# One decoder layer in fp32: bias products of the weight fold on VectorE, first token loads behind two weights, bias columns on ScalarE's queue

## The chip, the cores and the metric

The kernel runs on one core of one Trainium2 chip. A core has TensorE (matmuls, called PE in the profile), VectorE (DVE), ScalarE (ACT), GpSimd (POOL) and SyncE (SP), and 16 DMA engines that all its DMA queues share. The metric is the device time of one execution in microseconds, as a median over runs. All data are fp32. A matmul of fp32 operands appears in the trace as two passes, so that a product over four tiles of the contraction counts 8 there; a transpose through TensorE appears once.

## The reference

x is 16 sequences of 256 tokens of width 512. The layer adds three residual branches, each behind a layer norm: self attention with three softmaxes over one score matrix, a cross attention with 8 heads and relative positions over a window, and a feed-forward part in which each token picks one of 8192 experts in each of 8 heads. Only the first part matters here:

```python
Q = x @ Wq + bq
K = x @ Wk + bk
V = x @ Wv + bv
raw = jnp.einsum('bqd,bkd->bqk', Q, K) * scale
...  # three softmaxes over raw (causal, over means of 4 keys, over the top 64)
out = (w_attn + c_attn + s_attn) / 3.0
return out @ Wo + bo
```

Since raw = (x Wq + bq)(x Wk + bk)^T, the kernel needs from the two weights and the two biases only four things: the matrix Wq Wk^T (512 x 512), the column Wk bq, the row Wq bk, and the number bq . bk.

## The kernel before

The program has a short start, 19 rounds of attention that are pipelined over the 16 sequences, and an expert stage of 32 rounds. At the start weights are folded. First, with transposes through TensorE (jobs TQ and TK, four banks each), Wq and Wk are turned; ScalarE copies each bank to `raw_q` and `raw_k`. Then four products M build `w_qk` = Wq Wk^T, one bank of 512 columns each. Job C gives the column `b_g` = Wk bq and the number `bqk` from matmuls whose moving operand is 2 columns wide (`b_q2`, bq written twice), with the transposed Wk as the weights, and job U gives the row `u_row`, Wq bk, on all 128 partitions, from a copy of bk spread over 128 columns (`b_k_wide`) against the transposed Wq. The list `FOLD_JOBS` fixes the order of these jobs and so which of four PSUM banks (`s_bank`, of which two are named h_bank) each takes: job n waits until ScalarE has emptied job n - 4. TensorE goes on to TK, and then to M, only when ScalarE has emptied all four banks of the weight before.

After the fold each engine runs `rounds`: a fixed program of 32 steps for each round, in which every engine does its part in the order that `round_` lists. Round -1 has only the first half of self attention of sequence 0 (transposes of the normalised tokens, the products Q and RAW, then at step 16 the fold of Wv and Wo with the job BO, then V and CK). Its first transposes need nothing of the fold but TensorE's turn and the normalised tokens; ScalarE copies them to `xn_t` only after it has copied `u_row`. VectorE's product of the normalised tokens with `u_row` (L1156) gives a bias of each score row.

SyncE's queue issues, in order, Wq, Wk, the seven small bias columns (semaphore `first_in`, awaited by VectorE before its first copies), Wv, Wo and the other weights. GpSimd issues the tokens of sequences 0 and 1 (`x_in`, named xn_ring in the trace), between building the identity matrix and clearing some tiles, and then the first context `c_in`. In the start VectorE spreads the bias columns, computes the statistics of sequence 0 and normalises it (L1139). GpSimd then clears `probs` (L675), whose memory held the untransposed Wq and Wk (`w_q`, `w_k`; in the trace all of it is in_rows). At steps 17 and 18 of round -1 GpSimd adds the folded output bias to the tokens of sequence 0 (`add_bo`, L579), for which it waits for job BO; the power that gives sequence 1 its reciprocal deviations (L556) stands behind it in GpSimd's program, at step 26.

Of the kernel before, what the change touches and what calls it, by code (L numbers as in the profile page):

```python
# [20 lines left out]
ALU = mybir.AluOpType  # L21
# [3 lines left out]
P = 128  # L25
# [102 lines left out]
def attention_pass(nc, w, kept_stats, early, x3_dram, rows_in, rows_out, rows_laid, fold_dram):  # L128
# [115 lines left out]
    def a_job(b, kind, n=0):  # L244
        return jobs_before(a_jobs, b) + a_jobs(b).index((kind, n))

    FOLD_JOBS = ([("TQ", m) for m in range(KD)] + [("TK", m) for m in range(KD)] + [("M", m) for m in range(KD)]
                 + [("C", 0), ("U", 0)] + [("TV", m) for m in range(KD)] + [("W", m) for m in range(KD)]
# [8 lines left out]
    with ExitStack() as ctx:  # L257
# [29 lines left out]
        b_q2 = sb("b_q2", [P, KD, 2])  # L287
        b_k_wide, b_v_wide = (sb(f"b_{n}_wide", [P, KD, P]) for n in "kv")
        b_g = sb("b_g", [P, KD])
        u_row = sb("u_row", [P, D])  # L290
# [66 lines left out]
        wide_ready = sem("wide_ready")  # L357
        row_bias_ready = sem("row_bias_ready")
# [75 lines left out]
        def _(sp):  # L434
            for n, (tile, src) in enumerate(weights):
                sp.dma_start(tile, src.rearrange("(k p) n -> p k n", p=P)).then_inc(
                    first_weight[n] if n < N_EARLY else rest_in, 16)
                if n == N_EARLY - 1:
                    for column, col_src in columns:
                        sp.dma_start(column[:], col_src).then_inc(first_in, 16)  # L440
# [95 lines left out]
        def _(pool):  # L536
# [6 lines left out]
            for b in range(2):  # L543
                pool.dma_start(x_in[:, b, :, :], w["x"][b].rearrange("(t p) n -> p t n", p=P)).then_inc(
                    x_loaded[b], 16)
# [4 lines left out]
            after(nc.gpsimd.memset(band[:], 0.0))  # L550
            pool.dma_start(c_in[:], w["ctx"][0].rearrange("(t p) n -> p t n", p=P)).then_inc(c_loaded, 16)
# [87 lines left out]
            def round_(b, p):  # L639
                for s in range(STEPS):  # L640
# [21 lines left out]
                    if norm_in_round(b):  # L662
                        if s == At.LOAD_X and not (isinstance(b, int) and b == -1):
                            load_x(b + 2, p)
                        if s == At.POWER:
                            power(mom, rstd, 0, b + 2)
                        if 0 <= s - At.ADD_BO < TT:
                            add_bo(b + 2, p, s - At.ADD_BO)
                    if isinstance(b, int) and b == -1 and 0 <= s - At.LOAD_X < TT:
                        add_bo(0, 0, s - At.LOAD_X)  # L670
# [3 lines left out]
            pool.wait_ge(f_emptied, f_job("TK", KD - 1) + 1)  # L674
            nc.gpsimd.memset(probs[:], 0.0).then_inc(probs_zeroed, 1)  # L675
# [4 lines left out]
        def _(pe):  # L680
# [196 lines left out]

            def fold_scores():

                pe.wait_ge(first_weight[0], 16)  # L880
                turn_weight("TQ", w_q)
                pe.wait_ge(first_weight[1], 16)
                turn_weight("TK", w_k)
                for m in range(KD):
                    bank = f_open("M", m)
                    product(bank[:], lambda k: raw_q[:, k, m * P:(m + 1) * P], lambda k: raw_k[:, k, :],
                            KD).then_inc(f_filled, 1)
                pe.wait_ge(wide_ready, 1)
                bank = f_open("C")
                for m in range(KD):  # L890
                    product(bank[:, 2 * m:2 * m + 2], lambda k: raw_k[:, k, m * P:(m + 1) * P],
                            lambda k: b_q2[:, k, :], KD)
                product(bank[:, 2 * KD:2 * KD + 2], lambda k: b_k_wide[:, k, :], lambda k: b_q2[:, k, :],
                        KD).then_inc(f_filled, 1)
                bank = f_open("U")
                product(bank[:], lambda k: b_k_wide[:, k, :], lambda k: raw_q[:, k, :], KD).then_inc(f_filled, 1)
# [58 lines left out]
        def _(act):  # L955
# [120 lines left out]
            def fold_scores():  # L1076
                turn_weight("TQ", raw_q)
                turn_weight("TK", raw_k)
                for m in range(KD):
                    bank = f_full("M", m)  # L1080
                    nc.scalar.copy(w_qk[:, m, :], bank[:]).then_inc(f_emptied, 1)
                bank = f_full("C")
                nc.scalar.copy(b_g[:].unsqueeze(2), bank[:, 0:2 * KD].rearrange("p (m c) -> p m c", c=2)[:, :, 0:1])
                nc.scalar.mul(bqk[:], bank[:, 2 * KD:2 * KD + 1], SCALE).then_inc(f_emptied, 1)
                bank = f_full("U")
                nc.scalar.copy(u_row[:], bank[:]).then_inc(f_emptied, 1)
# [41 lines left out]

            fold_scores()
            act.wait_ge(first_in, 16 * N_FIRST_DMAS)  # L1130
            nc.scalar.mul(cb_qs[:], cb_q[:], XSCALE)
            self_wait(act)
            act.wait_ge(f_emptied, f_job("U") + 1)
# [3 lines left out]
        def _(dve):  # L1137
# [232 lines left out]
            nc.vector.tensor_copy(b_q2[:], b_q[:].unsqueeze(2).to_broadcast([P, KD, 2]))  # L1370
            nc.vector.tensor_copy(cb_v2[:], cb_v[:].unsqueeze(2).to_broadcast([P, CT, 2]))
            nc.vector.tensor_copy(b_k_wide[:], b_k[:].unsqueeze(2).to_broadcast([P, KD, P]))
            nc.vector.tensor_copy(b_v_wide[:], b_v[:].unsqueeze(2).to_broadcast([P, KD, P])).then_inc(wide_ready, 1)
            for t in range(TT):
                norm_stats(0, 0, t)
            for t in range(TT):
                norm_x(0, 0, t)
            dve.wait_ge(f_emptied, f_job("U") + 1)
# [564 lines left out]
```

## Time and profile before

| | us |
|---|---|
| Median of three runs | 2556.84 |
| Fastest and slowest of them | 2553.26, 2561.5 |
| Span of the profiled execution | 2553.4 |
| TensorE busy, share of the span | 2402.2 (94%) |
| VectorE busy | 2042.5 (80%) |
| ScalarE busy | 1121.9 (44%) |
| GpSimd busy | 1079.4 (42%) |

The span runs from the first to the last instruction. No other time is given for the profiled execution; its span lies beside the fastest of the three timed runs. Busy is time in which an engine had an instruction in it. In the rows further down the first number is the start of a group of like instructions in us from the span's start, the second is the time the group took; in square brackets stand the idle time of the engine before it and what ended that. Among the columns of a table of stretches, PEclk is the clock that TensorE was granted, as a share of 2.4 GHz. The fold ends at 44.55 us of the span.

### The profile page before, as it was taken

How to read it: one execution, taken by the hardware profiler on the slowest of the kernel's cores; microseconds unless marked ns; L12 is line 12 of the kernel's file. 1: busy time of each engine (PE TensorE's matmuls, PEld its weight loads, DVE VectorE, ACT ScalarE, POOL GpSimd, SP SyncE). 2: the span in 40 equal slices, each digit the busy share in tenths (PEclk: the TensorE clock that was granted, in tenths of full speed). 3: DMA queues.
4: the chain of work that ended last, by engine and by line, in shares of the span. 5: the costliest groups of instructions: out<-in, count | busy, mean ns of one | idle time of the engine just before them, and what ended most of it. 6: DMA issues, size and time to landing. Idle time of an engine off the chain costs nothing. (4 is left out here: it accounts for less than half of the span.)

```text
span 2553.4 us, 40781 instructions
## 1 busy us (share of the span) xinstructions
PE 2402.2 (94%) x12856; PEld 1333.3 (52%) x12856; DVE 2042.5 (80%) x5966; ACT 1121.9 (44%) x2612; POOL 1079.4 (42%) x1564
## 2 busy tenths in 40 slices
PE   7889999999999999999989899999999999999985
PEld 5456666656666566666555344444444444444432
DVE  1467776677767776677665699999999999999997
ACT  2257666667666666667666122222122222212221
POOL 1133333333333333334233445555555555555552
PEclk9999999999999999999999999999999999999998
DMA  3035554455545545455458789999999999999996
GB/s 112 15 108 139 163 151 141 134 148 149 155 125 144 162 143 155 114 145 172 135 148 258 272 337 390 392 382 384 382 382 383 385 389 391 383 383 382 385 371 261
DMA packets 292741, 622.47 MB, mean 244 GB/s; under 512 B 162352, under 2 KB 163376, under 8 KB 292528
## 3 DMA queue, kind: packets, MB, share of 16 engines
q0 software_dynamic: 83968, 438.34, 45.2%
q1 hardware_dynamic: 174768, 80.85, 11.9%
q10 hardware_dynamic: 33792, 100.67, 11.7%
q8 instruction: 105, 1.72, 0.3%
q14 instruction: 108, 0.88, 0.1%
HBM read 577.80 MB, written 142.61 MB: 282 GB/s over the span
## 5 line engine op out<-in xcount | busy, mean ns | idle before, releaser
L1544 POOL DMA_INDIRECT out_rows<-rows_out,rows_now x256 | 272.0, 1063 | 373.1 <-PE out_ps L1611 292.5
L1054 ACT ACTIVATE in_rows<-scores,nmx 128x512 f32<-128x512 f32 x512 | 373.2, 729 | 113.8 <-DVE nmx L1243 111.1
L1565 PE MATMUL l_bank<-fold,xn_tf 128*128 128x512 f32 x960 | 421.6, 592 | 0.0
L1060 ACT COPY in_rows<-t_bank 128x512 f32<-128x512 f32 x512 | 298.7, 584 | 214.7 <-PE t_bank L715 213.7
L1535 POOL DMA_INDIRECT in_rows<-rows_in,rows_now x248 | 303.2, 1223 | 128.9 <-DVE hid L1799 63.8
L622 POOL TENSOR_TENSOR added<-mask_add,band 128x136 f32<-128x136 f32 (+1 forms) x512 | 246.7, 483 | 256.4 <-DVE nmx L1243 255.0
L715 PE MATMUL t_bank<-ident,in_rows 128*128 128x128 f32 x2048 | 319.6, 281 | 10.1 <-ACT in_rows L1027 5.1
L715 PEld LDWEIGHTS t_bank<-ident,in_rows 128*128 128x128 f32 x2048 | 237.4, 143 | 171.6 <-issue 100.8
L683 PE MATMUL a_bank<-fold 128*128 128x256 f32 (+1 forms) x1024 | 303.9, 441 | 15.4 <-ACT fold L975 6.9
L1807 DVE CUSTOM_DVE_ANT_0 out_rows<-out_rows,hid 128x1024 f32<-128x1024 f32 x256 | 307.1, 1221 | 3.5 <-ACT hid L1668 3.5
L1655 ACT COPY sims<-l_bank 128x512 f32<-128x512 f32 x120 | 70.2, 585 | 537.2 <-PE l_bank L1565 516.9
L1565 PEld LDWEIGHTS l_bank<-fold,xn_tf 128*128 128x128 f32 x960 | 182.4, 190 | 229.6 <-issue 229.6
L1243 DVE CUSTOM_DVE_ANT_0 scores<-h_bank,added 128x512 f32<-128x512 f32 x256 | 174.6, 688 | 157.8 <-PE s_bank L705 146.3
L1607 PE MATMUL out_ps<-w_out,hid_t 128*128 128x512 f32 x512 | 229.8, 602 | 10.6 <-ACT hid_t L1690 10.6
L683 PEld LDWEIGHTS a_bank<-fold 128*128 128x128 f32 x1024 | 187.5, 191 | 91.5 <-issue 49.5
L1577 PE MATMUL hid_ps<-w_in,xn_kept 128*128 128x512 f32 x512 | 226.9, 596 | 7.5 <-ACTq L1710 6.0
L1799 DVE SCALAR_TENSOR_TENSOR hid<-in_rows,lin,hid 128x1024 f32<-128x1024 f32 x160 | 204.5, 1278 | 0.5
L621 POOL COPY added<-mask_add 128x128 f32<-128x128 f32 (+2 forms) x224 | 71.6, 319 | 314.5 <-DVE nmx L1243 302.7
L1243 DVE CUSTOM_DVE_ANT_0 scores<-s_bank,added 128x512 f32<-128x512 f32 x256 | 175.5, 686 | 33.0 <-ACT in_rows L1054 11.5
L1771 DVE CUSTOM_DVE_ANT_0 in_rows<-in_rows,xn_ring 128x512 f32<-128x512 f32 x256 | 161.2, 683 | 9.6 <-PEq L257 9.6
L1577 PEld LDWEIGHTS hid_ps<-w_in,xn_kept 128*128 128x128 f32 x512 | 97.8, 191 | 131.9 <-issue 131.9
L705 PE MATMUL h_bank<-in_rows 32*128 32x512 f32 x512 | 146.0, 647 | 17.2 <-DVE nmx L1243 14.7
(210 smaller groups left out, 3829.9 us busy)
## 6 DMA issues: line engine op xcount, KB each, us to landing
rows_in<-in_in_b_dram ACTq DMA_DIRECT2D x16, 2048.0 KB, 8.5
rows_out<-in_out_a_dram ACTq DMA_DIRECT2D x16, 2048.0 KB, 9.0
rows_in<-in_in_a_dram ACTq DMA_DIRECT2D x16, 1024.0 KB, 8.3
rows_out<-in_out_b_dram ACTq DMA_DIRECT2D x16, 1024.0 KB, 5.8
rel_scratch<-rel_pad SPq DMA_DIRECT2D x16, 640.0 KB, 3.2
band<-rel_scratch SPq DMA_DIRECT2D x512, 20.0 KB, 2.5
prob_scratch<-in_rows SPq DMA_DIRECT2D x512, 20.0 KB, 2.3
near<-prob_scratch SPq DMA_DIRECT2D x64, 156.1 KB, 3.1
```

What stands on the lines that cost most here:

```text
L622: nc.gpsimd.tensor_tensor(added[:, s % 2, lo:hi], mask[:, lo:hi], band[:, group % 2, g, lo - first:hi - first], ALU.add).then_inc(added_re ...
L683: ins = nc.tensor.matmul(out, lhs(k), rhs(k), start=(k == 0), stop=(k == k_tiles - 1 and not more))
L715: ins = nc.tensor.transpose(bank[:, k * P:(k + 1) * P], src[:, k * P:(k + 1) * P], ident[:])
L1054: nc.scalar.activation(prob_tile(s % PSLOTS), scores[:, s % 2, :], ACT.Exp, bias=nmx[:, s:s + 1], scale=-1.0, accum_out=lsum[:, s:s + 1]). ...
L1060: nc.scalar.copy(prob_t[:, n // HPT % 2, n % HPT, :, :].rearrange("p k q -> p (k q)"), bank[:]).then_inc(t_emptied, 1)
L1243: nc.vector.tensor_tensor_reduce(out=scores[:, s % 2, :], in0=s_bank[s % HPT][:, 0:L], in1=added[:, s % 2, :], scale=-1.0, scalar=-NEG, op ...
L1535: nc.gpsimd.indirect_dma_start(in_rows[:, place_in(h, odd), :], None, rows_in, bass.IndirectOffsetOnAxis(rows_now[:, odd, h:h + 1], 0)).th ...
L1544: nc.gpsimd.indirect_dma_start(out_rows[:, h, :], None, rows_out, bass.IndirectOffsetOnAxis(rows_now[:, odd, h:h + 1], 0)).then_inc(out_lo ...
L1565: ins = nc.tensor.matmul(l_bank[c % 2][:], xn_t[:, k, :], fold[:, k, c * BANK:(c + 1) * BANK], start=(k == 0), stop=(k == KD - 1))
L1577: ins = nc.tensor.matmul(hid_ps[:, n * BANK:(n + 1) * BANK], xn_kept[:, k, :], w_in[:, k, n * BANK:(n + 1) * BANK], start=(k == 0), stop=F ...
L1607: nc.tensor.matmul(out_ps[:], hid_t[:, k, :], w_out[:, k, :], start=(k == 0), stop=False, skip_group_check=True)
L1807: nc.vector.tensor_tensor_reduce(out=out_a[:, h, :], in0=out_a[:, h, :], in1=hid[:], scale=1.0, scalar=0.0, op0=ALU.mult, op1=ALU.add, acc ...
```

## The change

1. The jobs C and U no longer multiply. After the first M bank TensorE transposes spread copies of bq and bk (4 transposes each, jobs BQ and BK), which puts the bias as a row on every partition; ScalarE copies the two banks to `b_q_row` and `b_k_row`. VectorE multiplies the untransposed weights with those rows and sums along them: four instructions give `u_col`, four give `b_g`, one gives `bqk`. `u_col` is spread to 128 columns and TensorE transposes it (4 transposes, the new job U).
2. The bias columns are issued from ScalarE's queue, before its first work, and not from SyncE's behind Wk.
3. GpSimd issues the tokens and `c_in` after its clearing, and only once Wq and Wk have landed.
4. GpSimd's clearing of `probs`, and ScalarE's first copy of a round, wait for `columns_ready`, since the products read and overwrite the weights in that memory. The additions of the output bias for sequence 0 move from steps 17 and 18 behind the power at step 26.

```diff
-                 + [("C", 0), ("U", 0)] + [("TV", m) for m in range(KD)] + [("W", m) for m in range(KD)]
+    FOLD_JOBS = ([("TQ", m) for m in range(KD)] + [("TK", m) for m in range(KD)] + [("M", 0), ("BQ", 0), ("BK", 0)]
+                 + [("M", m) for m in range(1, KD)] + [("U", 0)] + [("TV", m) for m in range(KD)] + [("W", m) for m in range(KD)]
...
# SyncE
-                if n == N_EARLY - 1:
-                    for column, col_src in columns:
-                        sp.dma_start(column[:], col_src).then_inc(first_in, 16)
...
# GpSimd
-            for b in range(2):
-                pool.dma_start(x_in[:, b, :, :], w["x"][b].rearrange("(t p) n -> p t n", p=P)).then_inc(
-                    x_loaded[b], 16)
             after(nc.gpsimd.memset(rel_k4[:], 0.0))
...
             after(nc.gpsimd.memset(band[:], 0.0))
+            for i in range(N_EARLY):
+                pool.wait_ge(first_weight[i], 16)
+            for b in range(2):
+                pool.dma_start(x_in[:, b, :, :], w["x"][b].rearrange("(t p) n -> p t n", p=P)).then_inc(
+                    x_loaded[b], 16)
...
                         if s == At.POWER:
                             power(mom, rstd, 0, b + 2)
+                            if b == -1:
+                                for t in range(TT):
+                                    add_bo(0, 0, t)
...
-                    if isinstance(b, int) and b == -1 and 0 <= s - At.LOAD_X < TT:
-                        add_bo(0, 0, s - At.LOAD_X)
...
             pool.wait_ge(f_emptied, f_job("TK", KD - 1) + 1)
+            pool.wait_ge(columns_ready, 1)
             nc.gpsimd.memset(probs[:], 0.0).then_inc(probs_zeroed, 1)
...
# TensorE
+            def lay_row(kind, wide):
+                bank = f_open(kind)
+                for k in range(KD):
+                    ins = nc.tensor.transpose(bank[:, k * P:(k + 1) * P], wide[:, k, :], ident[:])
+                ins.then_inc(f_filled, 1)
...
-                pe.wait_ge(wide_ready, 1)
-                bank = f_open("C")
-                for m in range(KD):
-                    product(bank[:, 2 * m:2 * m + 2], lambda k: raw_k[:, k, m * P:(m + 1) * P],
-                            lambda k: b_q2[:, k, :], KD)
-                product(bank[:, 2 * KD:2 * KD + 2], lambda k: b_k_wide[:, k, :], lambda k: b_q2[:, k, :],
-                        KD).then_inc(f_filled, 1)
-                bank = f_open("U")
-                product(bank[:], lambda k: b_k_wide[:, k, :], lambda k: raw_q[:, k, :], KD).then_inc(f_filled, 1)
+                    if m == 0:
+                        pe.wait_ge(wide_ready, 1)
+                        lay_row("BQ", b_q_wide)
+                        lay_row("BK", b_k_wide)
+                pe.wait_ge(u_ready, 1)
+                lay_row("U", u_wide)
...
# ScalarE
+                    if m == 0:
+                        for kind, row in (("BQ", b_q_row), ("BK", b_k_row)):
+                            nc.scalar.copy(row, f_full(kind)[:]).then_inc(f_emptied, 1)
+                nc.scalar.copy(u_row[:], f_full("U")[:]).then_inc(f_emptied, 1)
...
+            for column, col_src in columns:
+                act.dma_start(column[:], col_src).then_inc(first_in, 16)
             fold_scores()
...
+            act.wait_ge(columns_ready, 1)
             act.wait_ge(f_emptied, f_job("U") + 1)
             rounds(round_)
...
# VectorE
+            dve.wait_ge(f_emptied, f_job("BK") + 1)
+
+            def against_row(weight, row, scale, column):
+                return nc.vector.tensor_tensor_reduce(out=weight, in0=weight, in1=row, scale=scale, scalar=0.0,
+                                                      op0=ALU.mult, op1=ALU.add, accum_out=column)
+
+            for m in range(KD):
+                against_row(w_q[:, m, :], b_k_row, 1.0, u_col[:, m:m + 1])
+            self_wait(dve)
+            nc.vector.tensor_copy(u_wide, u_col[:].unsqueeze(2).to_broadcast([P, KD, P])).then_inc(u_ready, 1)
+            for m in range(KD):
+                against_row(w_k[:, m, :], b_q_row, 1.0, b_g[:, m:m + 1])
+            against_row(b_k_row, b_q_row, SCALE, bqk[:]).then_inc(columns_ready, 1)
+            self_wait(dve)
             dve.wait_ge(f_emptied, f_job("U") + 1)
             rounds(round_)
```

TensorE's program of the fold, before (L874 are transposes of weights, L683 products, the last row begins round -1):

```order
L874 MATMUL s_bank<-ident,in_rows 128x128 x8
L683 MATMUL h_bank<-in_rows 128x512 x8
L683 MATMUL s_bank<-in_rows 128x512 x8
L683 MATMUL h_bank<-b_q,in_rows 128x2 x16
L683 MATMUL h_bank<-b_q,b_k_wide 128x2 x4
L683 MATMUL h_bank<-in_rows,b_k_wide 128x512 x4
L743 MATMUL a_bank<-ident,fold 128x128 x8
```

The same place now (L879 transposes of weights, L688 products, L887 the rows laid, of which "fold" is where the spread bq and the spread `u_col` lie):

```order
L879 MATMUL s_bank<-ident,in_rows 128x128 x8
L688 MATMUL h_bank<-in_rows 128x512 x4
L887 MATMUL h_bank<-ident,fold 128x128 x4
L887 MATMUL s_bank<-ident,b_k_wide 128x128 x4
L688 MATMUL s_bank<-in_rows 128x512 x4
L688 MATMUL h_bank<-in_rows 128x512 x8
L887 MATMUL s_bank<-ident,fold 128x128 x4
L748 MATMUL a_bank<-ident,fold 128x128 x8
```

The 24 matmuls of C and U are gone from between M and round -1; eight transposes stand behind the first M bank and four behind the last.

VectorE's program from its spreading of the biases to its first product of a round, before (ISA is the product with a sum along the row, and the row after it the write of the sum):

```order
L1372 COPY b_k_wide<-b_k 128x512
L1373 COPY b_v_wide<-b_v 128x512
L49 BN_STATS stats<-xn_ring 128x6 x2
L53 BN_AGGR mom<-stats 128x2 x2
L55 TENSOR_SCALAR mom<-mom 128x2
L1139 TENSOR_SCALAR fold<-xn_ring,mom,rstd 128x512 x2
L1156 ISA w_in,row_bias<-fold,u_row,bqk 128x512
```

The same place now (in_rows holds Wq and Wk, xn_kept the row of bk, xn_tf that of bq):

```order
L1384 COPY b_k_wide<-b_k 128x512
L49 BN_STATS stats<-xn_ring 128x6 x2
L53 BN_AGGR mom<-stats 128x2 x2
L55 TENSOR_SCALAR mom<-mom 128x2
L1150 TENSOR_SCALAR fold<-xn_ring,mom,rstd 128x512 x2
L1392 ISA in_rows,u_col<-in_rows,xn_kept 128x512
L1392 ISA u_col 128x1
...
L1398 COPY fold<-u_col 128x512
...
L1392 ISA xn_kept,bqk<-xn_kept,xn_tf 128x512
L1392 ISA bqk 128x1
L1167 ISA w_in,row_bias<-fold,u_row,bqk 128x512
```

Nine products L1392 have come in, four ahead of the spreading of `u_col` and five behind it; all stand behind the first statistics, which wait for the tokens of sequence 0, and the first of them waits until ScalarE has emptied job BK.

## Rows read from the trace of the kernel before

**Rows 1.** Busy time of each engine in stretches (start:end, length, engines, PEclk, DMA share, GB/s).

```profile
220.00:300.00 80.00, 76.83 (x615) 49.17 (x614) 57.91 (x190) 54.25 (x134) 29.48 (x63) 1.00 0.52 147
300.00:380.00 80.00, 76.83 (x615) 49.25 (x614) 58.07 (x188) 54.33 (x136) 29.79 (x63) 1.00 0.50 145
1400.00:2500.00 1100.00, 1060.01 (x2814) 482.96 (x2814) 1057.84 (x2863) 230.97 (x420) 586.49 (x541) 0.99 0.96 375
```

**Rows 2.** TensorE in order of time: start, time, line, operation, count [idle before, ended by].

```profile
6.71 1.94 PE L874 MATMUL h_bank<-ident,in_rows 128*128 128x128 f32 x8 [6.71 <-DMA in_rows<-in_attn_Wq_dram]
...
12.72 1.94 PE L874 MATMUL h_bank<-ident,in_rows 128*128 128x128 f32 x8 [2.36 <-issue]
...
17.04 9.61 PE L683 MATMUL h_bank<-in_rows 128*128 128x512 f32 x16 [0.67 <-ACT in_rows L1074]
26.48 7.03 PE L683 MATMUL s_bank<-in_rows 128*128 128x512 f32 x16
33.35 4.67 PE L683 MATMUL h_bank<-b_q,in_rows 128*128 128x2 f32 x32
...
39.58 5.13 PE L683 MATMUL h_bank<-in_rows,b_k_wide 128*128 128x512 f32 x8
44.55 0.60 PE L743 MATMUL a_bank<-ident,fold 128*128 128x128 f32 x4
...
60.40 1.04 PE L874 MATMUL s_bank<-ident,in_rows 128*128 128x128 f32 x8
...
77.32 3.60 PE L683 MATMUL s_bank<-in_rows,b_v_wide 128*128 128x512 f32 x8
...
96.30 0.60 PE L743 MATMUL a_bank<-ident,fold 128*128 128x128 f32 x4
```

**Rows 3.** Stretches around the end of the fold, columns as in Rows 1.

```profile
35.00:40.00 5.00, 5.00 (x27) 5.00 (x27) 0.00 (x0) 0.24 (x2) 0.00 (x0) 0.57 0.00 0
40.00:45.00 5.00, 5.00 (x12) 2.12 (x11) 0.00 (x0) 0.25 (x1) 0.00 (x0) 0.75 0.00 0
```

**Rows 4.** DMA issues of the start: size of one, us from issue to landing.

```profile
in_rows<-in_attn_Wq_dram SPq DMA_DIRECT2D x1, 1024.0 KB, 5.8
in_rows<-in_attn_Wk_dram SPq DMA_DIRECT2D x1, 1024.0 KB, 11.4
xn_ring<-in_x_dram POOLq DMA_DIRECT2D x2, 512.0 KB, 8.6
...
b_q<-in_attn_bq_dram SPq DMA_DIRECT2D x1, 2.0 KB, 11.3
...
cb_o<-in_xattn_bo_dram SPq DMA_DIRECT2D x1, 1.0 KB, 9.5
```

**Rows 5.** Two stretches of one us in the loading, columns as in Rows 1.

```profile
11.00:12.00 1.00, 0.00 (x0) 0.00 (x0) 0.00 (x0) 0.00 (x0) 0.00 (x0) 1.00 1.04 362
12.00:13.00 1.00, 0.28 (x2) 0.31 (x3) 0.00 (x0) 0.00 (x0) 0.00 (x0) 1.00 0.84 165
```

**Rows 6.** VectorE in order of time.

```profile
15.22 0.42 DVE L1372 COPY b_k_wide<-b_k 128x512 f32<-128x512 f32 x1
...
15.89 1.28 DVE L49 BATCH_NORM_STATS2 stats<-xn_ring 128x6 f32<-128x512 f32 x2
...
18.66 4.21 DVE L1139 TENSOR_SCALAR fold<-xn_ring,mom,rstd 128x512 f32<-128x512 f32 x2 [0.92 <-POOL rstd L556]
45.37 0.75 DVE L1156 CUSTOM_DVE_ANT_0 w_in<-fold,u_row,bqk 128x512 f32<-128x512 f32 x1 [22.50 <-ACT u_row L1086]
...
85.66 0.55 DVE L1139 TENSOR_SCALAR fold<-xn_ring,mom,rstd 128x512 f32<-128x512 f32 x1 [10.40 <-POOL rstd L556]
```

**Rows 7.** ScalarE in order of time, at the end of U.

```profile
44.75 0.59 ACT L1086 COPY u_row<-h_bank 128x512 f32<-128x512 f32 x1 [4.76 <-PE h_bank L683]
...
45.57 0.58 ACT L975 COPY fold<-a_bank 128x512 f32<-128x512 f32 x1
```

**Rows 8.** GpSimd in order of time, the clearing and the first output bias.

```profile
18.59 3.55 POOL L675 MEMSET in_rows<- 128x4160 f32 x1
...
82.48 2.48 POOL L579 TENSOR_TENSOR xn_ring<-xn_ring,b_o 128x512 f32<-128x512 f32 x2 [20.07 <-ACT b_o L1094]
```

More of the change, by code:

```diff
@@ L245, in a_job @@
         return jobs_before(a_jobs, b) + a_jobs(b).index((kind, n))
-    FOLD_JOBS = ([("TQ", m) for m in range(KD)] + [("TK", m) for m in range(KD)] + [("M", m) for m in range(KD)]
-                 + [("C", 0), ("U", 0)] + [("TV", m) for m in range(KD)] + [("W", m) for m in range(KD)]
+    FOLD_JOBS = ([("TQ", m) for m in range(KD)] + [("TK", m) for m in range(KD)] + [("M", 0), ("BQ", 0), ("BK", 0)]
+                 + [("M", m) for m in range(1, KD)] + [("U", 0)] + [("TV", m) for m in range(KD)] + [("W", m) for m in range(KD)]
                  + [("BO", 0), ("RT", 0), ("RV", 0)])
@@ L286, in attention_pass @@
         b_q, b_k, b_v = (sb(f"b_{n}", [P, KD]) for n in "qkv")
-        b_q2 = sb("b_q2", [P, KD, 2])
         b_k_wide, b_v_wide = (sb(f"b_{n}_wide", [P, KD, P]) for n in "kv")
+        b_q_wide, u_wide = (part(early.fold, (14 + i) * D, KD, P) for i in range(2))
+        b_q_row, b_k_row = (part(tile, 0, D) for tile in (early.xn_t, early.xn_kept))
         b_g = sb("b_g", [P, KD])
+        u_col = sb("u_col", [P, KD])
         u_row = sb("u_row", [P, D])
@@ L357, in attention_pass @@
         wide_ready = sem("wide_ready")
+        columns_ready = sem("columns_ready")
+        u_ready = sem("u_ready")
         row_bias_ready = sem("row_bias_ready")
@@ L1081, in fold_scores @@
                     nc.scalar.copy(w_qk[:, m, :], bank[:]).then_inc(f_emptied, 1)
[L1082 to L1086, printed above, removed]
+                    if m == 0:
+                        for kind, row in (("BQ", b_q_row), ("BK", b_k_row)):
+                            nc.scalar.copy(row, f_full(kind)[:]).then_inc(f_emptied, 1)
+                nc.scalar.copy(u_row[:], f_full("U")[:]).then_inc(f_emptied, 1)
             def fold_values():
@@ L1369, in _ @@
             dve.wait_ge(first_in, 16 * N_FIRST_DMAS)
-            nc.vector.tensor_copy(b_q2[:], b_q[:].unsqueeze(2).to_broadcast([P, KD, 2]))
             nc.vector.tensor_copy(cb_v2[:], cb_v[:].unsqueeze(2).to_broadcast([P, CT, 2]))
-            nc.vector.tensor_copy(b_k_wide[:], b_k[:].unsqueeze(2).to_broadcast([P, KD, P]))
-            nc.vector.tensor_copy(b_v_wide[:], b_v[:].unsqueeze(2).to_broadcast([P, KD, P])).then_inc(wide_ready, 1)
+            nc.vector.tensor_copy(b_v_wide[:], b_v[:].unsqueeze(2).to_broadcast([P, KD, P]))
+            nc.vector.tensor_copy(b_q_wide, b_q[:].unsqueeze(2).to_broadcast([P, KD, P]))
+            nc.vector.tensor_copy(b_k_wide[:], b_k[:].unsqueeze(2).to_broadcast([P, KD, P])).then_inc(wide_ready, 1)
             for t in range(TT):
```

## The prediction

> **What bounds the kernel now.** I read the busy times by stretch first. From 220 to 380 us two neighbouring stretches of 80 us show the same 76.83 us of TensorE, 615 passes each, with VectorE at 58: the attention rounds repeat exactly, so what happens at the start is not made up for there; it moves them all. The expert stage, 1400 to 2500 us, has VectorE busy 1057.84 of 1100 us beside DMA at 0.96, and starts when the rounds end [rows 1]. Neither has an absolute date. So the time of the kernel is that of the start plus a chain that hangs on it, and the change touches only the start.
>
> Then TensorE in order of time [rows 2]. It waits 6.71 us for Wq; 16 transposes; idle 2.36 us until 12.72; 16 transposes; idle 0.67 us for ScalarE's last copy; M from 17.04 to 33.35; C from 33.35 to 39.58, of passes only 2 columns wide; U from 39.58 to 44.55; then round -1. From 6.71 on TensorE has a gap only for Wk and for ScalarE's copies. The start is TensorE's chain, with the loads in front of it. VectorE is idle for 22.50 us before its product at 45.37, which waits for `u_row` [rows 6]: there is room beside M for vector work.
>
> The clock comes third. The PEclk column has 1.00 before 30 us, yet eight transposes take 1.94 us at 6.71 and 1.04 at 60.40, and the first 16 passes of M take 9.61 us against 7.03 for the second 16 [rows 2]. So TensorE ran at 1.2 GHz up to a point within M: a pass costs 0.43 us at full clock (6.87 / 16, from 26.48 to 33.35) and 0.86 at half, the first 16 took 9.44 from start to start, so about 6 of them were slow, and the clock rose at 17.04 + 6 x 0.86 = 22.1 us. While C ran, whose array work is small for its time, the grant fell: 0.57 in 35 to 40 us and 0.75 in 40 to 45 [rows 3]. U paid for it: 8 passes in 5.0 us against 3.60 for a product of the same form at 77.32 [rows 2].
>
> **The change, part by part.**
>
> Removed: C (39.58 - 33.35 = 6.23 us) and U (44.55 - 39.58 = 4.97 us), 11.20 us of TensorE's chain [rows 2]. U's share holds 1.4 us that C's low clock had caused.
>
> Added on TensorE: BQ and BK, 8 transposes: 0.87 us at full clock (1.04 for a group of eight with its tail, 60.40), 1.73 at half [rows 2]. M's first bank is 8 passes, which by the rates above end just at the rise of the clock, so I take 0.9. The new U is 4 transposes; the row at 44.55 has 0.60 for four with the tail [rows 2], I take 0.5. Together 1.4 us, and 2.6 if all were slow.
>
> The new waits. The row products begin when ScalarE has emptied BK: M's first bank ends at about 16 + 6.0 = 22, the transposes at 23, ScalarE's three copies of 0.58 [rows 7] begin behind the first of these, so 24. Four products at 0.75 and a spread at 0.42 [rows 6] give `u_ready` at about 27.6, five more products give `columns_ready` at 31.4. TensorE asks for `u_ready` at about 33.3, behind M, and ScalarE for `columns_ready` at about 34.5. Slack 5.7 and 3 us: no cost. The products could not hide if each cost over 2 us, or began over 5 us late. Behind the waiting transposes on TensorE stands the whole of round -1, so a late `u_ready` would be paid in full.
>
> What could start them late is the tokens, since the products stand behind their statistics on VectorE. GpSimd now issues them when Wk has landed, about 10.5 us. They took 8.6 us to land while sharing the engines with Wk [rows 4]; the same again gives 19.1 us. Statistics to the first normalisation took 18.66 - 15.89 = 2.8 us, and the pair 4.21 us, against 0.55 for one at 85.66 [rows 6]: GpSimd's clearing lay beside the pair (18.59 to 22.1) [rows 8], and it now waits for `columns_ready`. So VectorE is free at 19.1 + 2.8 + 1.1 = 23.0, or at 26.1 at the old price, ahead of 24 or 2 us behind it; `u_ready` is then at 29.7 at the latest, still 3.6 us early. GpSimd's clearing itself (3.55 us) now ends near 35; it is needed by ScalarE in round 1, over 100 us on.
>
> Loads. Before, Wk took 11.4 us to land beside the tokens, Wq 5.8 [rows 4]. With the tokens out of the way Wk's 1024 KB need some 2.9 us after Wq at the 362 GB/s of the undisturbed stretch [rows 5]: landed at 10.3, while TensorE, done with Wq, asks at 7.4 + 4.3 = 11.7. The 2.36 us gap goes, but 0.67 of it stays, as the wait for ScalarE's copies that the next weight shows; from 12.72 to 17.04, 4.32 us, is the price of one weight with that wait. Against it stand the bias columns, which now pass with Wq, not behind Wk. When they passed before, the rate fell from 362 to 165 GB/s for a us [rows 5]: 0.54 us lost. The upper bound is the time over which they landed: b_q was issued first and took 11.3, cb_o last and took 9.5 [rows 4]; if the two groups of issue and landing kept their distance, about 2 us; the lower is 0. I take 0.7, near the row on the rate.
>
> The Trainium skill, page DMA: Bandwidth & Descriptors, section Issuing engines are not separate DMA queues, says that transfers of SP's, ACT's and POOL's queues run on the same 16 engines and interleave, and that another issuing engine saves only its issue time. By that rule moving the columns to ScalarE's queue saves Wq nothing and can only delay it; taken alone it would put the term anywhere from 0 to 2 us of loss, and the row on the rate chooses within that. The trace agrees so far as Wk and the tokens go: 11.4 us against Wq's 5.8 [rows 4].
>
> The output bias of sequence 0 behind the power: VectorE waits 10.40 us for that power before 85.66, because GpSimd sits 20.07 us on job BO until 82.48 [rows 6, 8]. That wait goes. It is worth nothing by itself: what waits for this normalisation are the transposes at 96.30, over 9 us after it, and TensorE reaches them out of its own products [rows 2]. The bounds are 0 and, if VectorE's later work were on the path, 10.4; I take 0.
>
> **The sum.** M begins at 6.71 + 0.7 + 2 x 4.32 = 16.05, against 17.04. M takes the same 16.31 us if the clock rises as long after M's start as before, and 0.5 more if it rises at the same point of the span. Round -1 begins at 16.05 + 16.31 + 0.9 + 0.5 = 33.8, or 34.3, where it began at 44.55: a gain of 10.8 or 10.3; I take 10.5. Behind it ScalarE's first copy of the round follows at the same distance, since `u_row` and its neighbours stand in the same order (44.75 to 45.57) [rows 7]. Made against the profiled span this is 2553.4 - 10.5 = 2542.9 us. That span is 3.4 us (0.13%) under the median of the three runs shown and 0.2 over the fastest, so against the median: 2556.84 - 10.5 = 2546.3 us. What a comparison of this kernel can tell from no change is about 0.3%, 7.7 us; the forecast lies 2.8 us beyond that.
>
> **Rivals.**
>
> *The clock rises earlier.* Before, TensorE stood idle for 2.36 us between the two weights; now 32 transposes run with 0.7 us gaps straight into M. If that is enough for the full clock by M's start, the 6 slow passes of M cost 2.6 us less, and the last transposes shrink as well, though ScalarE's copies then set their pace. Gain 13, time 2543.8. Against it: the transposes from 12.72 on, with M at once behind them, did not raise the clock before 22.1. The Trainium skill, page TensorE: Matmul & The Clock Gate, section What's actually happening, says that the default is the lower clock and that the rise is not tied to the kernel's own start, so that it varies between runs. By that the same kernel would show gains on both sides of 10.5; one trace cannot show it.
>
> *The head gives the gain back.* The columns cost Wq 2 us, not 0.7; the clock rises later against M, so that four more passes are slow (1.7 us); BQ and BK run at half clock (0.9). Gain 10.5 - 1.3 - 1.7 - 0.9 = 6.6, time 2550.2, which counts as no change. For it: the columns are many small packets beside the one load that TensorE waits for.
>
> *The change does not do what it says*: the tokens land so late that TensorE waits for `u_ready`. `u_ready` comes 3.9 + 3.4 us behind their landing, so they would have to land after 26 us for a first loss and at 36.4 for all of the gain, where 8.6 us after the issue is 19.1. If they landed near 30, the time would be 2550.
>
> *Slower.* TensorE loses its full clock for longer later on. The rest of the start has short products and gaps, and its whole timing against the clock's decisions moves by 10.5 us. A us at half clock costs 0.5 us where TensorE is the bound. It takes 21 us of further half clock to eat the gain and 36 us for a loss of 0.3%. In the fold before, about 7 us were low ((1 - 0.57) x 5 and (1 - 0.75) x 5 us, doubled) [rows 3], behind passes 2 columns wide, and these are just what goes. At 36 us the time is 2564.5.
>
> **How the numbers follow.** Forecast 50%, with its own range 2542 to 2551; early clock 17%; gain given back 23%; late tokens 5%; slower 5%. Of the forecast's own cases some 85% lie beyond 7.7 us of gain, of the early clock's nearly all, of the given-back gain's a third, of the late tokens' few: faster 68%, within 0.3% 27%, slower 5%. The range takes in the early clock and most of the given-back gain, and leaves the ends of both out: 2541 to 2554.
>
> **What would show it.** In the trace after: the transposes of Wq at about 7.4 (6.7: the columns cost nothing), those of Wk at 11.7 behind ScalarE and no longer behind the DMA, M at about 16, round -1's first transposes at 34 with no idle time before them, the row products between 24 and 31.5 at 0.75 us each, TensorE never waiting for `u_ready`, and no fall of PEclk at that place. Wrong would be: idle time on TensorE before the new U, Wq landing past 9 us, products well above 1 us, or round 1 beginning by less than 9 us earlier although round -1 did; then the gain was lost between them.

## The result and the profile after

| | us |
|---|---|
| Median before, 6 runs | 2553.01 (2550.15 to 2561.5) |
| Median after, 6 runs | 2541.61 (2535.98 to 2542.34) |
| Ratio after to before | 0.995, 95% interval 0.9939 to 0.9961 |
| Profiled spans | 2553.4 before, 2540.4 after |

The change makes the kernel 11.4 us faster by the medians and 12.8 by the ratio (10.0 to 15.6). The forecast was 10.5 us. Two more groups of runs of the same two kernels gave 0.995 and 0.9954. But the trace after shows that the sum was not made of the terms that I had put into it. Below, "the head" is the stretch from the start to round -1's first transposes, and M, C and U are the jobs of the fold.

TensorE in order of time, in the trace after (answers to [rows 2]):

```profile
6.73 1.94 PE L879 MATMUL h_bank<-ident,in_rows 128*128 128x128 f32 x8 [6.73 <-DMA in_rows<-in_attn_Wq_dram]
8.46 1.55 PE L879 MATMUL s_bank<-ident,in_rows 128*128 128x128 f32 x8
10.69 1.09 PE L879 MATMUL h_bank<-ident,in_rows 128*128 128x128 f32 x8 [0.68 <-ACT in_rows L1083]
...
13.49 3.70 PE L688 MATMUL h_bank<-in_rows 128*128 128x512 f32 x8 [0.83 <-ACT in_rows L1083]
17.02 0.60 PE L887 MATMUL h_bank<-ident,fold 128*128 128x128 f32 x4
...
21.33 7.03 PE L688 MATMUL h_bank<-in_rows 128*128 128x512 f32 x16
28.20 0.60 PE L887 MATMUL s_bank<-ident,fold 128*128 128x128 f32 x4
28.64 0.60 PE L748 MATMUL a_bank<-ident,fold 128*128 128x128 f32 x4
```

Read the durations first. The first eight transposes still take 1.94 us; the next eight 1.55; Wk's eight take 1.09. So the clock rose within Wq's transposes, at about 9.5 us, where it had risen within M at 22.1 before. Every pass of M then runs at full clock: M without the two laid rows between takes 28.20 - 13.49 - 0.88 = 13.8 us against 16.3. Round -1 begins at 28.64, 15.9 us before the 44.55 of before. Taken apart: C and U less the three laid rows 11.2 - 1.3 = 9.9; M 2.5; the idle time before Wk 1.7; Wk's transposes 1.7. The small rest is Wq's transposes, 0.4 sooner, less a wait before M that is 0.2 longer. The span fell by 13.0, so the later stages took 2.9 us more.

The loads, in the trace after (us to landing; answers to [rows 4]):

```profile
in_rows<-in_attn_Wq_dram SPq DMA_DIRECT2D x1, 1024.0 KB, 5.9
in_rows<-in_attn_Wk_dram SPq DMA_DIRECT2D x1, 1024.0 KB, 8.2
...
xn_ring<-in_x_dram POOLq DMA_DIRECT2D x2, 512.0 KB, 7.3
...
cb_o<-in_xattn_bo_dram ACTq DMA_DIRECT2D x1, 1.0 KB, 7.4
```

After its issue Wk lands 3.2 us sooner, Wq as before: the columns beside Wq cost it nothing that can be seen. VectorE and ScalarE in the trace after (answer to [rows 6, 7]):

```profile
17.05 1.29 DVE L49 BATCH_NORM_STATS2 stats<-xn_ring 128x6 f32<-128x512 f32 x2 [3.96 <-DMA xn_ring<-in_x_dram]
...
19.83 1.00 DVE L1150 TENSOR_SCALAR fold<-xn_ring,mom,rstd 128x512 f32<-128x512 f32 x2 [0.92 <-POOL rstd L559]
20.75 0.69 DVE L1392 CUSTOM_DVE_ANT_0 in_rows<-in_rows,xn_kept 128x512 f32<-128x512 f32 x1
...
23.35 0.43 DVE L1398 COPY fold<-u_col 128x512 f32<-128x512 f32 x1
...
26.14 0.69 DVE L1392 CUSTOM_DVE_ANT_0 xn_kept<-xn_kept,xn_tf 128x512 f32<-128x512 f32 x1
```

```profile
28.40 0.59 ACT L1090 COPY fold<-h_bank 128x512 f32<-128x512 f32 x1 [2.85 <-PE h_bank L688]
28.88 0.59 ACT L1094 COPY u_row<-s_bank 128x512 f32<-128x512 f32 x1
...
29.72 0.58 ACT L984 COPY fold<-a_bank 128x512 f32<-128x512 f32 x1
```

The products are hidden as planned: spread by 23.8 where TensorE asks at 28.2, the last sum at 26.8 where ScalarE asks at 29.72. The pair of normalisations takes 1.00 us and not 4.21, with GpSimd's clearing now behind it. TensorE has no idle time before the new U.

### The profile page after: what moved, and what is told of

It reads as the page before. It is cut to its first block and busy times, and to the rows that moved or that the text cites. A ratio compares the mean times of both kernels' runs of the same rounds, so it can differ in the third digit from the quotient of the medians.

```text
span 2540.4 us, 40733 instructions
## 1 busy us (share of the span) xinstructions
PE 2385.6 (94%) x12820; PEld 1323.5 (52%) x12820; DVE 2048.2 (81%) x5985; ACT 1122.8 (44%) x2612; POOL 1080.6 (43%) x1564
## 5 line engine op out<-in xcount | busy, mean ns | idle before, releaser
L688 PE MATMUL a_bank<-fold 128*128 128x256 f32 (+1 forms) x1024 | 303.0, 440 | 15.2 <-ACT fold L984 6.6
L688 PEld LDWEIGHTS a_bank<-fold 128*128 128x128 f32 x1024 | 187.5, 191 | 90.5 <-issue 48.5
```

What stands on the lines that cost most here:

```text
L688: ins = nc.tensor.matmul(out, lhs(k), rhs(k), start=(k == 0), stop=(k == k_tiles - 1 and not more))
```

## The experiments

"The changed kernel" is the one above, in its three groups of runs. All ratios are to the kernel before; those of one group were run on the same chip.

### The parts alone

**Products alone** (e1_products): the changed kernel with these parts of the diff undone.

```diff
# SyncE, GpSimd, ScalarE: columns behind Wk, tokens early, add_bo at steps 17 and 18 as before
-            for column, col_src in columns:
-                act.dma_start(column[:], col_src).then_inc(first_in, 16)
-            for i in range(N_EARLY):
-                pool.wait_ge(first_weight[i], 16)
```

> The row products, the laid rows and their waits alone; the loads and the order of GpSimd's output bias as before. Theory A (the gain is mostly the work taken from TensorE's chain): C and U cost 11.2 us before, the laid rows 1.3 to 1.4, so 9.8 us less than before (2543), whatever the clock does in the head; round -1 begins 9.9 us nearer to M's start than before. Rival B (the loads and what they do to the clock carry half of it or more): under 7 us less. Rival C (the early rise of the clock in the head belongs to this part): the clock is up before M although the idle time between the two weights is still there.

Measured: 2546.61 us, ratio 0.9976 (0.9965 to 0.9986), 6.1 us less. The 9.8 of theory A are just outside the interval; rival B's under 7 fits the ratio, but the interval reaches to 8.9. The trace has round -1 at 33.62. Rival C fails, in a way that I had not foreseen: the clock rose at 10.8 us and fell again at 14.2, behind the idle time for Wk, so that it was not up when M began; and the kernel before, without this part, can rise as early (before_again, below).

**Both loads alone** (e2_loads), the kernel before with columns and tokens moved, C and U kept.

> The loads alone: bias columns on ScalarE's queue, tokens behind the two weights; C and U stay. Theory A: the idle time of 2.4 us between the weights shrinks to 0.7, so 1.7 us less than before, which a comparison of whole runs barely shows; 2.6 to 4.3 us more where the clock happens to rise early. Rival B: 5 us or more less, in every run. If the clock rises early only because TensorE's gap is gone, the trace shows transposes of the first weight still at 0.23 us each and those of the second faster.

2548.73 us, ratio 0.9984 (0.9974 to 0.9993), 4.1 us less (1.8 to 6.6). In its trace the clock is up at 9.8 us, Wk's eight transposes take 1.10 us and round -1 begins at 38.56: the case for which theory A had 1.7 and 2.6 to 4.3 more. The interval takes in both that and rival B's 5. **Tokens alone** (e4_tokens):

```diff
+            for i in range(N_EARLY):
+                pool.wait_ge(first_weight[i], 16)
+            for b in range(2):
+                pool.dma_start(x_in[:, b, :, :], ...   # behind the clearing, not ahead of it
```

> Only the tokens moved behind the two weights; the columns stay on SyncE's queue behind Wk. Theory A: Wk lands near 10 us, TensorE's idle time before it goes from 2.4 to 0.7, 1.7 us less than before. Rival: C now waits for nothing new, but the columns and VectorE's spreading come later and delay nothing either; if they do, TensorE has idle time before C.

2547.04 us, ratio 0.9974 (0.9963 to 0.9985), 6.6 us less (3.8 to 9.4), where theory A had 1.7. **Columns alone** (e3_columns):

> Only the bias columns moved to ScalarE's queue; tokens as early as before. Wq's landing: 6.7 us if the columns cost nothing beside it (as in the trace of the changed kernel), up to 8.7 by the bound of the prediction. Wk still lands at about 12.6, beside the tokens, since their sharing is what delayed it. Theory A: time as before within 2 us. Rival: the columns were what delayed Wk; then it lands 1 us or more earlier here.

2553.02 us, ratio 0.9999 (0.9988 to 1.0009): nothing. In its trace the rows of the two weights read (the last column is us to landing):

```profile
in_rows<-in_attn_Wq_dram SPq DMA_DIRECT2D x1, 1024.0 KB, 6.0
in_rows<-in_attn_Wk_dram SPq DMA_DIRECT2D x1, 1024.0 KB, 12.3
```

So the tokens, and not the columns, had delayed Wk. Beside early tokens the columns delay it a little further: it lands 12.0 to 12.3 us after its issue in the three traces with both (e3, e11, e12) and 11.4 to 11.9 in the six with early tokens alone. The parts, products and both loads, give 6.1 and 4.1 by ratio, 10.2 together, where the whole gave 12.8 (10.0 to 15.6); with the tokens alone in place of both loads it would be 12.7. Within intervals of some 2.5 us either way on each part they add up, and no closer statement can be made.

**Output bias back at steps 17 and 18** (e5_addbo_back), all else changed.

> The changed kernel with the output bias of sequence 0 back at steps 17 and 18, ahead of the power. Theory A: VectorE idles some 10 us again before its normalisation in round -1, TensorE's rows stay where they are, time as the changed kernel (2541 within 2 us). Rival: this wait was on the path in part; then this kernel is 3 to 10 us slower than the changed one.

2538.87 us, ratio 0.9945 (0.993 to 0.9961), as the changed kernel; the upper end of its interval is 2.8 us above the changed kernel's 0.995. VectorE waits again, and TensorE's rows behind it show the same waits as in the changed kernel:

```profile
69.97 0.55 DVE L1149 TENSOR_SCALAR fold<-xn_ring,mom,rstd 128x512 f32<-128x512 f32 x1 [10.29 <-POOL rstd L559]
```

### Is the slack of the products what the trace says?

**Twelve more products** (e8_late12):

```diff
+            for _ in range(12):
+                nc.vector.tensor_tensor_reduce(out=part(early.fold, 15 * D, D), in0=b_k_row, in1=b_k_row, scale=1.0,
+                                               scalar=0.0, op0=ALU.mult, op1=ALU.add, accum_out=u_col[:, 0:1])
+                self_wait(dve)
             for m in range(KD):
                 against_row(w_q[:, m, :], b_k_row, 1.0, u_col[:, m:m + 1])
```

> The changed kernel with 12 more row products of the same form (with a wait for their end) on VectorE ahead of the four for u_col; their sums are thrown away. At 0.61 us from start to start and some 0.15 for the wait they cost 9 us. In the trace of the changed kernel u_ready was 4.4 us early and columns_ready 2.9. Theory A: 9 - 2.9 = about 6 us slower than the changed kernel, with 4.7 us of idle time on TensorE before the new U. Rival: the start has more slack than that, since round -1 can catch up; then under 3 us slower.

2549.88 us, ratio 0.9982 (0.9974 to 0.9991): 8.2 us behind the changed kernel by ratio, of which 7.3 are seen in its trace (0.4 of them because M began that much later):

```profile
34.03 1.11 PE L887 MATMUL s_bank<-ident,fold 128*128 128x128 f32 x4 [5.25 <-DVE fold L1402]
```

```profile
37.06 0.59 ACT L984 COPY fold<-a_bank 128x512 f32<-128x512 f32 x1 [1.19 <-DVE bqk L1392]
```

37.06 against 29.72: the delay passes in full, there is no catching up. Theory A holds, with 5.25 us of idle time where 4.7 were expected. The four transposes at 34.03 take 1.11 us and not 0.60: the granted clock fell to half at 31.3 us, within that idle time.

### The clock

**Fillers in front** (e6_warm_before, e7_warm_after): 20 transposes of the identity while TensorE waits for Wq.

```diff
             pe.wait_ge(consts, 1)
+            for _ in range(20):
+                nc.tensor.transpose(s_bank[3][:, 0:P], ident[:], ident[:])
             fold_scores()
```

> The kernel before, with 20 transposes of the identity into an unused bank while TensorE waits for Wq; their result is overwritten. If an active TensorE raises the clock, it is up when Wq's transposes begin or during them, and M's 32 passes all run at 0.43 us: 2.6 us less on M, up to 1.4 on the transposes of Wk; 2 to 4 us less than before in every run. Rival D (the moment of the rise has nothing to do with the work in front of it): as before.

> The changed kernel with the same 20 transposes in front. If the profiled run of the changed kernel already rose early by chance, its median holds runs of both kinds, and this kernel is 1 to 3 us faster in the median, M at 13.2 us or earlier in its trace. If the early rise belongs to the changed kernel in every run, this one equals it within 1 us.

In the kernel before (e6) it gained nothing: 2555.58 us, 1.0003 (0.9992 to 1.0013). Its trace says why: Wq's transposes run at full clock, then TensorE idles 4.59 us for Wk, and Wk's run at half clock:

```profile
7.63 1.04 PE L874 MATMUL s_bank<-ident,in_rows 128*128 128x128 f32 x8
13.26 1.94 PE L874 MATMUL h_bank<-ident,in_rows 128*128 128x128 f32 x8 [4.59 <-issue]
```

In the changed kernel (e7): 2538.23 us, 0.9933 (0.992 to 0.9947), 4.3 us better than 0.995 by ratio, but the intervals overlap, and e5_addbo_back, which was as fast as the changed kernel, had 2538.87 beside it. Round -1 begins at 27.55, 1.1 us sooner.

**Again, unchanged** (before_again, before_third, after_again, after_third), since one trace can't show chance.

> The kernel before once more, for a second trace of its head. If the moment of the rise is chance, it can rise at about 10 us (then it falls again behind the idle time for Wk) or as late as 22. Round -1 begins at 41 to 46 us.

> The kernel before, a third trace of its head: round -1 at 41 to 46 us; where the clock rises near 10 us it falls at about 13.

> The changed kernel, unchanged, for a second look at its head and beside the kernels of this group. If the moment at which the clock rises is chance, it can be at 10 us again or as late as 20; round -1 then begins at 28.6 or up to 4 us later. Time 2538 to 2543.

> The changed kernel once more, beside e11 and e12: 2538 to 2543; the clock up before Wk's transposes and round -1 from 28.6 us on, or up to 3.5 us later if the rise comes late.

The same program gives two kinds of head. In before_again (span 2548.2) the clock rose at 10.0 us and M ran fast, in before_third (2557.4) it rose at 22.6, as in the trace of before. The first 16 passes of M, in before_again and then in before_third:

```profile
17.02 7.13 PE L683 MATMUL h_bank<-in_rows 128*128 128x512 f32 x16 [0.68 <-ACT in_rows L1074]
```

```profile
17.48 9.65 PE L683 MATMUL h_bank<-in_rows 128*128 128x512 f32 x16 [0.67 <-ACT in_rows L1074]
```

In before_again the PEclk of 10 to 15 us has 0.84: the clock fell at 13.4, behind the idle time, and was back at 16.8, for M.

```profile
10.00:15.00 5.00, 2.18 (x13) 2.01 (x12) 0.00 (x0) 1.56 (x4) 0.00 (x0) 0.84 0.99 320
```

after_again (2540.77 us, 0.995, interval 0.9934 to 0.9966) and after_third (2541.41 us, 0.9954, interval 0.9939 to 0.9969) both rose at 9.5 to 9.9 us and did not fall before round -1, at 28.80 and 28.60. Of the seven traces with late tokens and no fillers only e4_tokens rose late, at 19.3. In the six with early tokens and no fillers the clock rose early and fell again in three (before_again, e1, e3) and rose only within M in three (before, before_third, e11).

**Filling the idle time** (e10_fill_before): 20 fillers in front and 38 between the weights, in the kernel before.

```diff
                 turn_weight("TQ", w_q)
+                for _ in range(38):
+                    nc.tensor.transpose(acc, ident[:], ident[:])
                 pe.wait_ge(first_weight[1], 16)
```

> The kernel before with 20 transposes of the identity ahead of Wq and 38 more between the weights, into a bank that nothing uses yet; their results are never read. They fill the time in which TensorE waits for Wk and change no load. In all three traces with early tokens in which the clock had risen before Wk (products alone, columns alone, 20 transposes in front), it fell again at 12 to 14 us, behind that idle time. Theory E (the idle time for Wk makes the clock fall, and this is what the moved tokens really save): the clock stays up here, Wk's transposes take 0.11 us each and M 13.7 us; round -1 begins near 42 and the time is 2 to 4 us below before. Rival F (the fall has another cause): it falls at 12 to 14 us here too, and the time is as before or, as the fillers then take twice as long, some us above.

Its trace is as theory E has it: no fall, M in 13.8 us, round -1 at 40.15, 2 to 5 us ahead of the three traces of before. Its time is not: 2553.7 us, 1.0 (0.999 to 1.0011), so a gain above 2.6 us is excluded (one of the twelve runs took 3550.11 us and is not in the ratio). Theory E holds in the head and not in the time, and that is the reason for the last pair: **tokens early in the changed kernel**, without (e11_tokens_back) and with 20 and 34 fillers (e12_tokens_back_fill).

> The changed kernel with the tokens issued as early as before; nothing else is undone. Wk lands at about 13.5 us as with the columns alone. Theory E (late tokens save the idle time for Wk and the fall of the clock behind it): 3 us of idle time and 1.5 to 2.6 us of slow work come back, so 4 to 6 us slower than the changed kernel. Rival G (only the idle time counts): 3 us slower at most.

> The kernel of e11 with 20 transposes of the identity in front of Wq and 34 between the weights, their results never read; the loads stay as in e11. Theory E: the clock stays up to M and beyond, M's 32 passes take 13.7 us, and this kernel is 1.5 to 2.6 us faster than e11. Rival G: as e11 within 1 us.

| | us | ratio (95%) | round -1 begins |
|---|---|---|---|
| after_third | 2541.41 | 0.9954 (0.9939 to 0.9969) | 28.60 |
| e11, tokens early | 2545.95 | 0.9972 (0.9961 to 0.9983) | 34.80 |
| e12, tokens early, idle time filled | 2539.61 | 0.9949 (0.9936 to 0.9963) | 31.22 |

Wk's transposes and M's first bank in e11:

```profile
13.26 1.94 PE L877 MATMUL h_bank<-ident,in_rows 128*128 128x128 f32 x8 [2.98 <-issue]
...
17.59 5.76 PE L686 MATMUL h_bank<-in_rows 128*128 128x512 f32 x8 [0.68 <-ACT in_rows L1081]
```

and in e12, behind the fillers:

```profile
9.53 3.93 PE L893 MATMUL acc_bank<-ident 128*128 128x128 f32 x34 [0.83 <-ACT in_rows L1085]
13.30 1.07 PE L877 MATMUL h_bank<-ident,in_rows 128*128 128x128 f32 x8
```

Wk lands late in both. In e11 the clock did not fall behind the idle time: it rose only at 21.8, within M. With TensorE kept busy (e12) Wk's transposes take half the time and round -1 comes 3.6 us sooner, 1.5 on those transposes and 2.1 on M. The whole kernel gains 5.9 us by ratio, more than the 1.5 to 2.6 of theory E, and the slowest run of e12 (2540.8) is ahead of the fastest of e11 (2542.49). Rival G falls.

What late tokens gave the head can now be split. From e11 to after_third, one trace each, it is 6.2 us: 3.6 of the clock, and 2.6 because Wk's transposes begin at 10.65 and not at 13.26. By time e12 can't be told from the changed kernel, but its fillers in front help it too. Against e7, which has the same 20 in front and late tokens, its head is 3.7 us longer and its ratio 0.9949 against 0.9933, with intervals that overlap. So the wait for Wk isn't shown to be free once the clock is held; by the heads the clock is the larger part of the two.

**A better version** (e9_best): the changed kernel, 22 fillers, and the wait for all of Wq's banks taken out ahead of Wk's transposes.

```diff
-                pe.wait_ge(f_emptied, f_job(kind, KD - 1) + 1)
+                if kind != "TQ":
+                    pe.wait_ge(f_emptied, f_job(kind, KD - 1) + 1)
```

> The changed kernel with 22 transposes of the identity in front of Wq, and without the wait for ScalarE's last copy of Wq before Wk's transposes (each bank still waits for its own copy). The clock is up before Wq's second bank in every run; M begins at 12 us or a little before, against 13.5, round -1 at 27 us. 1.5 to 3 us less than the changed kernel in the median.

```profile
6.74 1.09 PE L879 MATMUL h_bank<-ident,in_rows 128*128 128x128 f32 x8 [0.56 <-DMA in_rows<-in_attn_Wq_dram]
...
9.73 1.09 PE L879 MATMUL h_bank<-ident,in_rows 128*128 128x128 f32 x8 [1.02 <-DMA in_rows<-in_attn_Wk_dram]
...
12.53 3.70 PE L688 MATMUL h_bank<-in_rows 128*128 128x512 f32 x8 [0.83 <-ACT in_rows L1086]
```

2536.74 us, 0.9933 (0.9917 to 0.9949), the lowest median; after_again beside it had 2540.77, 0.995. 4 us by the medians, with intervals that overlap. TensorE now waits for Wk's landing again (1.02 us), so the waits between the banks are no longer what holds it. Nor did taking the wait out gain anything that the head shows: e7, with fillers and with that wait, begins round -1 at 27.55, e9 at 27.68. No run has the wait taken out without fillers.

### Does the head's gain reach the end?

| trace | round -1 begins | span | span less that | half clock behind it |
|---|---|---|---|---|
| before_third | 45.05 | 2557.4 | 2512.3 | 73.8 |
| before | 44.55 | 2553.4 | 2508.9 | 73.8 |
| before_again | 42.10 | 2548.2 | 2506.1 | 60.1 |
| e3_columns | 41.14 | 2554.3 | 2513.2 | 80.1 |
| e4_tokens | 40.79 | 2547.2 | 2506.5 | 60.1 |
| e1_products | 33.62 | 2545.0 | 2511.4 | 69.8 |
| e12_tokens_back_fill | 31.22 | 2538.7 | 2507.5 | 66.5 |
| after | 28.64 | 2540.4 | 2511.7 | 76.7 |
| after_again | 28.80 | 2537.8 | 2509.0 | 63.5 |
| e9_best | 27.68 | 2533.1 | 2505.4 | 59.6 |

The last column sums, in us, the stretches behind the start of round -1 in which the trace grants half the clock. Over all 18 traces (the table has ten) a fitted line gives 1.03 us of span for a us of the head, with a standard error of 0.10: what the head gains reaches the end. What is left varies between 2505.4 and 2513.2 and goes with the half clock, some 0.3 us for each us of it (correlation 0.81; no run changed that half clock by itself). The 2.9 us that the trace of after seemed to give back are of this kind: in after_again, of the same program, it is 0.1.

## Why the prediction was right and wrong

**Right.** The sign and, partly by luck as shown below, the size (10.5 against 11.4 and 12.8). What bounds the kernel and that a shift of the start passes to the end. The row products beside M at 0.69 us each, u_ready and columns_ready well ahead of what asks for them; the rival of late tokens did not come about. The wait of 10.40 us on VectorE was worth nothing that e5 can show. Wk's landing at 9.4 (10.3 forecast), and ScalarE's copies as the next wait. The laid rows, 1.3 us (1.4).

**The step that failed is the one on the loads**, "The 2.36 us gap goes, but 0.67 of it stays", priced at 1.7 less 0.7 for the columns, with 4.32 us per weight and 16.31 for M kept from the trace of before. Both loads together are worth 4.1 us (1.8 to 6.6), tokens alone 6.6 (3.8 to 9.4), in the changed kernel 4.5 by medians. In the trace after Wq takes 3.96 us, Wk 2.80 and M 13.8, and round -1 begins at 28.64 where the sum had 33.8 or 34.3. The columns cost Wq nothing (6.73 against 6.71), so that the us at 165 GB/s, from which I had taken the 0.7, did not show their cost. The larger part is the clock: in before_again, e1, e3 and e6, where it was up before the idle time for Wk, it fell within or just behind it; where there was no idle time and it had risen, it stayed up until round -1, or in the kernels with C and U until those (e8 apart, where it fell in the later wait that its twelve products make); and e12 gets 5.9 us back by fillers, with the loads unchanged. I had the early rise as a rival with 17%, and argued against it from a trace in which the clock simply had not risen yet. It is the usual case with late tokens and no fillers: 6 of 7 traces, e4 aside.

**The products' term went the other way.** 9.8 were forecast; the heads agree (e1 and e11 begin round -1 at 33.6 and 34.8, the four traces with C, U, early tokens and no fillers at 41.1 to 45.1), but whole runs give 6.1 (3.6 to 8.9) for e1 and 7.1 (4.3 to 10.0) for e11, which also moves the columns. The 9.8 are just outside the first interval and inside the second. So, as far as these runs tell, the two errors partly cancelled in the sum, which is luck. C and U took 11.2 us in all three traces of before and in e2, 9.6 in e3, e4 and e10, and 12.9 in e6, according to when the clock fell under them. With 9.6 the term would be 8.3, inside both intervals, but no trace of before had 9.6. Why the whole runs show less than the heads is open; so is why e10, whose head is about 2 us or more ahead of any trace of before, is no faster in time.

**The rival of more half clock later on** had the right size per us (0.3 measured, 0.5 taken as a bound where TensorE is the bound), and it goes with most of what makes single traces disagree; it did not decide the sign. The page TensorE: Matmul & The Clock Gate of the Trainium skill, section What's actually happening, says that the rise is not tied to the kernel's own start. The three traces of before, with a rise at 22.1, 10.0 and 22.6 us in one and the same program, agree. The page DMA: Bandwidth & Descriptors of the Trainium skill, section Issuing engines are not separate DMA queues, says that transfers end up on the same 16 DMA engines whichever engine started them. The runs agree: columns alone on another queue gave 0.9999.

## What to carry to other kernels

Before pricing idle time of TensorE by its length, look at what stands behind it: where the clock was up, a wait of 2.7 to 4.6 us for a load lost it for the transposes or products after it. Filling the wait with idle transposes brought 3.6 us of the head and 5.9 of the whole in the changed kernel with early tokens, but 2 us or more of the head and nothing of the whole in the kernel before: measure it. Load first what the first engine needs next and nothing beside it; issuing small transfers from another queue neither gained nor cost anything measurable alone. Compare heads in more than one trace before a term is taken from a duration at half clock, and measure the parts alone: here a right sum hid one term that was too small and one that was too large.

## What the runs showed of the hardware

- The PEclk column shows 1.00 from the start of the trace to the first record of the clock, though the first transposes run at half speed: eight take 1.94 us there and 1.04 to 1.09 at full clock. Durations decide there.
- The first rise comes at 9.5 to 10.8 us in 9 and at 19.3 to 22.6 us in 4 of the 13 traces without fillers in front, also for one and the same program (10.0, 22.1, 22.6). In e4 it came at 19.3 though TensorE had worked from 6.8 on with no gap above 0.7 us.
- A normalisation of 512 columns on VectorE took 3.76 us beside GpSimd's clearing and 0.55 without it. The pair took 4.21 us in before, before_again, e2, e3 and e4, with the clearing beside it, and 1.00 in after, e1 and e11, where the clearing comes later.
- Tokens issued beside the second weight delay it: Wk lands 11.4 to 12.3 us after its issue with them (nine traces, before, e3 and e11 among them), 8.1 to 8.5 without (nine, after and e4 among them).
